# A causal mask that moves from TensorE matmuls to a minimum on VectorE

## The reference

```
qk = x @ W_qk ; q, k = split(qk)            # 16 heads of 64, n = 1024
scores = einsum('bhid,bhjd->bhij', q * 64**-0.5, k)
scores = where(triu(ones(n, n), k=1), -max_float, scores)
attn = softmax(scores)
out = einsum('bhij,bhjd->bhid', attn, k)    # the keys are the values
x = x + out @ W_out
```

## Time and profile before

| | us |
|---|---|
| median of 3 runs (lowest to highest) | 827.27 (824.65 to 827.36) |
| profiled execution: its own time | 827.14 |
| its span, first to last instruction | 825.4 |
| busy: TensorE / VectorE / ScalarE / GpSimd | 740.8 / 462.3 / 390.0 / 439.0 |

### The profile page before, as it was taken

How to read it: one execution, slowest core, us unless ns; L and a number is a source line. 1 busy time by engine, 2 the same in 40 slices (tenths; PEclk the granted TensorE clock), 3 DMA queues, 4 the chain that set the end, 5 groups by cost and what they waited for, 6 DMA issues and landing times. The chain is left out here.

```text
span 825.4 us, 14251 instructions
## 1 busy us (share of the span) xinstructions
PE 740.8 (90%) x5448; PEld 495.9 (60%) x5448; DVE 462.3 (56%) x1232; ACT 390.0 (47%) x483; POOL 439.0 (53%) x316
## 2 busy tenths in 40 slices
PE   2789999999999999999999989988998856679998
PEld 2456555655555565556556547867887522657787
DVE  5765565666556556655755501555455774655343
ACT  2345556555555555555555441355444740255422
POOL 4356775676667658656855680044343553144343
PEclk9699999999999999999999999999999885899999
DMA  2000000000000000000000006132231000033232
GB/s 64 8 1 1 9 1 1 8 1 2 8 1 2 7 2 1 8 2 1 2 1 26 2 1 147 27 120 87 66 104 39 0 1 0 0 106 113 67 106 77
DMA packets 29459, 25.15 MB, mean 30 GB/s; under 512 B 10128, under 2 KB 20944, under 8 KB 29392
## 3 DMA queue, kind: packets, MB, share of 16 engines
q1 hardware_dynamic: 29392, 24.25, 10.1%
HBM read 22.92 MB, written 1.31 MB: 29 GB/s over the span
## 5 line engine op out<-in xcount | busy, mean ns | idle before, releaser
L378 POOL TENSOR_TENSOR all_x<-all_x,at_probs 128x1024 f32<-128x1024 f32 (+3 forms) x128 | 222.9, 1741 | 35.7 <-ACT at_probs L453 21.0
L453 ACT ACTIVATE at_probs<-at_ring 128x1024 f32<-128x1024 f32 x144 | 147.3, 1024 | 113.8 <-PE at_ring L625 107.3
L498 DVE CUSTOM_DVE_ANT_0 at_ring<-at_ring,at_after_query 128x128 f32<-128x128 f32 (+3 forms) x256 | 119.5, 521 | 74.1 <-PE at_ring L590 74.1
L643 PE MATMUL at_out<-at_probs,at_k_nat 128*64 128x512 f32 (+3 forms) x768 | 140.3, 494 | 1.1 <-DVE a_attn_t L521 0.9
L1079 POOL TENSOR_TENSOR m_prod<-m_gate,m_wb 128x512 f32<-128x512 f32 x64 | 81.8, 1283 | 110.6 <-ACT m_gate L936 85.5
L378 POOL TENSOR_TENSOR all_x<-at_probs 128x768 f32<-128x768 f32 (+1 forms) x32 | 66.9, 2091 | 126.5 <-ACT at_probs L453 126.3
L990 DVE TENSOR_TENSOR m_hid<-m_prod,m_u 128x512 f32<-128x512 f32 x64 | 44.0, 687 | 88.7 <-POOL m_prod L1079 84.4
L643 PEld LDWEIGHTS at_out<-at_probs,at_k_nat 128*64 128x64 f32 x768 | 49.2, 136 | 69.9 <-issue 66.0
L494 DVE TENSOR_REDUCE at_half_max<-at_ring 128x2 f32<-128x1024 f32 x64 | 75.5, 1222 | 12.4 <-PE at_ring L590 12.4
L936 ACT ACTIVATE m_gate<-m_g 128x512 f32<-128x512 f32 x72 | 42.9, 599 | 82.2 <-PE m_g L847 81.7
L855 PEld LDWEIGHTS m_acc<-rest_wd,m_hid 128*128 128x128 f32 x576 | 75.9, 194 | 6.2
(11 more groups left out here) (196 smaller groups left out, 1293.4 us busy)
## 6 DMA issues: line engine op xcount, KB each, us to landing
m_wb<-m_wt_far SPq DMA_DIRECT2D x128, 128.0 KB, 2.9
all_x<-in_L_attn_a_x SPq DMA_DIRECT2D x8, 256.0 KB, 3.7
at_w_raw<-in_L_attn_a_W_qk SPq DMA_DIRECT2D x8, 128.0 KB, 2.6
out<-all_x SPq DMA_DIRECT2D x4, 256.0 KB, 2.3
a_room<-in_L_attn_a_W_out SPq DMA_DIRECT2D x1, 512.0 KB, 4.0
m_raw_wg<-in_L_ffn_experts_wg SPq DMA_DIRECT2D x1, 512.0 KB, 4.8
m_raw_wu<-in_L_ffn_experts_wu SPq DMA_DIRECT2D x1, 512.0 KB, 4.2
rest_wd<-in_L_ffn_experts_wd SPq DMA_DIRECT2D x1, 512.0 KB, 4.2
```

Source lines behind the costliest of these rows:

```text
L378: return pool.tensor_tensor(sums[:, :, a * P:b * P], left, right, ALU.add)
L453: act.activation(probs[:, :, slot * BANK:(slot + 1) * BANK], pair("S", unit, slot)[:, :, :], ACT.Exp, scale=BETA).then_inc(exp_done, 1)
L498: last = dve.tensor_tensor_reduce(out=sums_ps, in0=sums_ps, in1=after_query[:, BANK - w:BANK], scale=1.0, scalar=MASKED, op0=ALU.add, op1= ...
L643: last = pe.matmul(out_ps[rows(l), o:o + (b - a) * P], k_nat[g % 3][:, j, rows(l)], probs[:, l, at:at + (b - a) * P], start=(j == 0), stop ...
```

## The change

Nothing is added to the scores any more. The tiles `eye2` and `mask2` go, and a constant tile `cap` of [128, 128] f32 is made at the start: 3e38 where the query isn't before the key, 0 elsewhere. After the exponential of a slot with a diagonal block, VectorE takes the minimum of that block's probabilities (both heads, [128, 2, 128]) and `cap`, in place. A new semaphore `capped` counts the slots so treated; `add_up` and `outputs` wait for it. VectorE does slot 0 in round 0, slot 1 after the first maxima of round 1, slot 2 after the maxima of round 2, and slots 7 and 8 in round 4 between `scale_out` and `max_rows`. The denominators of the first half and their inversion move from round 3 to round 4.

```diff
+DIAGONAL = [slot for slot in range(NSLOT) if any(a == j for j, a, _ in SLOTS[slot])]
...
-        eye2, mask2 = s.sb("eye2", [P, 2, P], BF16), s.sb("mask2", [P, 2, P], BF16)
+        cap = s.sb("cap", [P, P])
...
+        capped = s.sem("capped")
...
+        def caps(unit, slot):
+
+            return len(DIAGONAL) * unit + sum(d <= slot for d in DIAGONAL)
...
         def set_up(pool):
             split_w(pool, 0)
-            pool.memset(eye2[:, :, :], 0.0).then_inc(consts, 1)
-            pool.memset(mask2[:, :, :], 0.0).then_inc(consts, 1)
+            pool.memset(cap[:, :], -MASKED).then_inc(consts, 1)
             pool.memset(neg_pick[:, :], 0.0).then_inc(consts, 1)
             pool.memset(after_query[:, :], 0.0).then_inc(consts, 1)
-            pool.wait_ge(consts, 4)
+            pool.wait_ge(consts, 3)
...
+            pool.affine_select(out=cap[:, :], in_=cap[:, :], compare_op=ALU.is_ge, fill=0.0,
+                               base=0, pattern=[[1, P]], channel_multiplier=-1).then_inc(consts, 1)
...
             for l in range(2):
-                pool.affine_select(out=eye2[rows(l), :, :], in_=eye2[rows(l), :, :], compare_op=ALU.not_equal, fill=1.0,
-                                   base=0, pattern=[[DH, 2], [-1, P]], channel_multiplier=1).then_inc(consts, 1)
-                pool.affine_select(out=mask2[rows(l), :, :], in_=mask2[rows(l), :, :], compare_op=ALU.is_ge, fill=MASKED,
-                                   base=0, pattern=[[DH, 2], [-1, P]], channel_multiplier=1).then_inc(consts, 1)
...
                 def add_up(unit, n):
 
                     pool.wait_ge(exp_done, NSLOT * unit + SUM_NEEDS[n] + 1)
+                    pool.wait_ge(capped, caps(unit, SUM_NEEDS[n]))
...
-                        if r == 3:
+                        if r == NBURST - 1:
                             invert(unit, 0)
...
+                def cap_diagonal(unit, slot):
+
+                    dve.wait_ge(exp_done, NSLOT * unit + slot + 1)
+                    for seg, (j, a, _) in enumerate(SLOTS[slot]):
+                        if a == j:
+                            own = part(slot, seg, a, a + 1)
+                            last = dve.tensor_tensor(own, own, cap[:, :].unsqueeze(1).to_broadcast([P, 2, P]), ALU.min)
+                    last.then_inc(capped, 1)
...
                             if unit:
                                 scale_out(unit - 1, 0)
+                            cap_diagonal(unit, 0)
                             if more:
                                 queries_low(unit + 1)
                         for what, m in row:
                             if what == "M" and more:
                                 maxima(unit + 1, m)
+                            if (what, m) == ("M", 0):
+                                cap_diagonal(unit, 1)
+                        if r == 2:
+                            cap_diagonal(unit, 2)
                         if r == NBURST - 1:
                             if more:
                                 join_maxima(unit + 1)
                             if unit:
                                 scale_out(unit - 1, 1)
+                            cap_diagonal(unit, 7)
+                            cap_diagonal(unit, 8)
                             if more:
                                 max_rows(unit + 1)
...
-                        for h in range(2 if a == j else 0):
-                            for l in range(2):
-                                pe.matmul(to[l][:, 0:P], mask2[rows(l), h, :], eye2[rows(l), h, :], start=False, stop=False)
...
                     pe.wait_ge(exp_done, NSLOT * g + max(slot for slot, _ in BURSTS[r]) + 1)
+                    pe.wait_ge(capped, caps(g, max(slot for slot, _ in BURSTS[r])))
...
-                        if r == 3:
+                        if r == NBURST - 1:
                             denominators(unit, 0)
```

More of the change, by code:

```diff
@@ L524, in _ @@
                 queries_low(0)
-                dve.wait_ge(consts, 11)
+                dve.wait_ge(consts, 7)
                 for m in range(NMAX):
@@ L661, in _ @@
                 turn_keys(0)
-                pe.wait_ge(consts, 11)
+                pe.wait_ge(consts, 7)
                 pe.wait_ge(cleared, 4)
```

## The result

| us | before | after |
|---|---|---|
| median of 4 (lowest to highest) | 827.32 (824.65 to 829.17) | 864.50 (862.95 to 865.83) |
| profiled execution: its own time | 827.14 | 865.08 |
| its span | 825.35 | 863.33 |

The kernel became slower: 1.0436 times the time before (1.0416 to 1.0457). The prediction was 844.6, range 818 to 852. The direction is as forecast and so are the waits on VectorE, GpSimd and TensorE; the size is twice the forecast, mainly because the granted clock of TensorE also fell, which the forecast doesn't have.

What follows compares the result with a forecast made beforehand. PE was taken to bound the kernel, busy 28.32 of a unit's 28.76 us. Added to 827.14: units 1 to 13 +10.9, unit 0 +3.2, unit 14 +2.4, last unit +1.0, together 17.5, giving 844.6 us, range 818 to 852.

Steps and rivals of the forecast that it cites:

- the masks' price on PE: Mask matmuls on PE: 0.18 to 0.19 us per 512-wide block, 1.40 us a unit.
- M3: Fill 3 of the maxima on PE: starts 0.70 us early; t counts from the unit's first score matmul.
- cap 2: VectorE's minimum on slot 2, behind the maxima of round 2: ends at t = 14.93.
- sum 7: Step 7 of GpSimd's eleven sums: ends at t = 25.26, with no hole left between sums.
- cap 7: VectorE's minimum on slot 7: blocked at the SBUF port by sum 7, about 1.6 us long, ending at t = 25.54.
- sum 8: Step 8 of GpSimd's eleven: gets in between the halves of cap 8, t = 25.7 to 28.1.
- cap 8: VectorE's two minima on slot 8: second half waits for sum 8, about 2.4 us, to t = 28.4, delaying m_rows.
- Rivals 1, 2 and 3: VectorE holds port through cap 8: 816-824, 0.18; no port conflict: 808-816, 0.08; gains and losses cancel: within 4 of 827, 0.07.
- rival 4: The masks' gap on PE is refilled, nothing saved up to M3, the chain 0.70 later: 854 us, chance 0.06.
- Unit 0: Attention's first unit, without older outputs on PE: VectorE-GpSimd chain ends near 29.1 instead of 25.9 us, +3.2.
- The last unit: Attention's end, where PE waits for GpSimd's last sum: sums end about 1 us later, +1.0.
- Units 1 to 13: 13 x 0.84 = 10.9: Steady attention units: PE waits for m_rows, so each takes 29.6 instead of 28.76 us, +0.84.

Runs made afterwards that it cites:

- e1: Kernel before, with the mask matmuls left out and nothing in their place (output not the reference's): 813.98 us, 0.984.
- e2: Changed kernel with 14 extra 512-column matmuls on PE ahead of each unit's first scores: 849.45 us, 1.026.
- e5: Kernel before, masks kept, with m_rows delayed by eight reductions of a constant on VectorE: 861.82 us, 1.0405.
- e9: e5 with one more reduction, of 128 elements, ahead of max_rows: 868.05 us (857.93 to 875.81).
- e10: e5 with a ninth 512-element reduction: 881.78 us (876.14 to 900.2).
- e3: Changed kernel with slot 8's two minima in one VectorE instruction: 828.65 us, 1.0003.
- e8: Changed kernel, each slot's minima in one instruction, slot 2's earlier, sum 8 waiting for cap 8, second half's denominators and inversion in round 2: 815.46 us, 0.9846.
- e6: e3 with the second half's denominators and their inversion moved from round 1 to round 2: 816.01 us, 0.9848.
- e4: Changed kernel with m_rows computed ahead of the minima of slots 7 and 8 on VectorE: 842.24 us, 1.0177.

## Why the prediction was wrong

- Right: the masks' price on PE. From L640 to what follows L642 a 512-wide masked slot now takes 0.46 us (forecast 0.47), and M3 starts at t = 11.50 (11.36). PE was not ready as early as forecast, though: at t = 28.1 (29.89 - 1.79), not 27.7, and e1 says that of the 1.05 us a unit that PE could have gained only 0.88 would have stayed.
- Right: the minimum at 0.41 to 0.42 us (0.42); cap 2's end at t = 15.07 (14.93); sum 7's end at 25.58 (25.26); cap 7's end at 25.87, 1.92 us long (25.54, "about 1.6"); sum 8 between the halves of cap 8 in every unit, from 26.00 to 28.43 (25.7 to 28.1); m_rows' end at 29.84 (29.55); PE waiting 1.8 us (1.9; this agreement is in part luck, as m_rows ends 0.3 us later than forecast and PE is ready 0.4 us later). Rivals 1, 2 and 3 are out by this, and rival 4 by the 0.46. The Trainium skill, page "SBUF — State Buffer", section "Who interferes with whom", has issue order decide and the first to issue hold the port for its whole length; the trace agrees (222.04 before 222.16, 2.43 us whole).
- Small misses: cap 2 ends 0.14 us late and GpSimd's gaps between sums are 0.17 us, not 0.14, so that sum 7 ends 0.3 us late; the steady unit is +1.14 without the clock, not +0.84: 3.9 us in 13 units. Unit 0 (+3.0 for 3.2) and unit 14 (+2.8 for 2.4) hold. The last unit was given +1.0 and took +4.3: its sums start 1.9 us later than before, and it has two stretches at half clock, behind a wait of 3.35 us for m_rows and one of 4.04 for the scaling. In e2, without the first of these stretches and with 3.4 us instead of 6.8 in the other, the last unit is 1.6 us longer than before; so some 2.7 of the 4.3 go with the clock.
- **The step that failed:** "Units 1 to 13: 13 x 0.84 = 10.9." It measured 27.8. The term prices PE's new wait at its length and lets the work behind it run as in the window of before, "at full granted clock". In 8 of the 14 units 1 to 14 the granted clock was 0.50 for 3.4 us or more behind that wait, which cost 1.5 us a unit (2.4 in unit 1). e2 shows it by itself: the same chain on VectorE and GpSimd, the same 29.9 us, the wait filled, no alternation, and 15 us less. With that term added (13.0 in these units, some 2.7 in the last) the sum would have been about 860; the 3.9 above are most of what is then left.
- A sign of it stood in the earlier trace rows: the window of unit 0, with PE busy 23.81 of 25.90 us, has a mean clock of 0.94, beside 1.00 in a unit without holes. I read the busy times of that row and not its clock. The trace of before also shows where in that window: right behind the one wait of PE for m_rows, 2.6 us long, the granted clock is 0.51 for 3.4 us, after 1.00 in the 3.3 us before. PE's wait (total, times, longest), then that window:

```profile
PE at_ring L616 <- DVE at_m_rows L512: 2.6, 1, 2.6
...
42.50:45.90 3.40, 3.40 (x15) 2.15 (x16) 0.00 (x0) 0.91 (x1) 0.00 (x0) 0.51 0.00 0
```

  The profile of before couldn't give the frequency, but it could give a bound: 0.06 x 25.9 = 1.55 us lost in that window, and as much at each of the 15 waits would have put the range's high end near 844.6 + 23 = 868.

The Trainium skill, page "TensorE: Matmul & The Clock Gate", section "HAM oscillation — how this bites in real kernels", tells of a kernel where a wait between groups of matmuls throws the clock back to its lower level at every group. The traces here agree in kind, but not in "every": 9 of 15 waits in the changed kernel, 3 of 15 in e5.

What stays open is what decides which waits are followed by a fall. It isn't the length alone: waits of 1.6 us were followed by a fall in 2 of 13 units (e5), of 1.8 in 7 of 13 with the masks gone and in none of e9's profiled execution, of 2.2 in 3 of 12 (e10). Nor is it the absence of the masks alone (units 2 to 14 of e1, e3 and e8 have no such wait and no fall). No run moves a wait of one length in time, so it is untested whether its moment matters.

## What to carry to other kernels

Price a new wait on TensorE twice: its length, and the stretch at half clock that may follow; here the stretches cost 13.0 us in 13 units, nearly as much as all the rest of the change there (14.8 us: the waits' 23.5, less what PE gained), and where a wait can't be avoided, work that is thrown away may be cheaper than idling (e2). Between two short VectorE instructions that read SBUF twice, a long GpSimd sum that has just been released gets in: put them in one instruction, or release the sum behind them (e3, e8). A change that looks bad in its net time can hold a good part: the mask on VectorE is 1.5% faster than on TensorE (1.3 to 1.8, by the intervals of e6 and e8) once two details of order are mended.

## What the runs showed of the hardware

- After waits of PE of 1.6 to 4.0 us the granted clock was 0.50 for 3.4 us in some cases (6.8 at some waits of 2.6 us and more), in which 512-column matmuls take 0.63 us instead of 0.40; 3.4 us of it cost a unit 1.5 us. Waits of 0.92 and 0.46 us in one unit (e4) were followed by none.
- Whether it happens varies from wait to wait within one execution: of the 13 waits of 1.62 to 1.65 us in e5, two were followed by a fall. Whether it varies from execution to execution isn't shown; the four executions of the changed kernel agree within 2.9 us.
- Two minima of 256 elements back to back cost 0.41 and 2.58 us with a sum released between them, one of 512 costs 0.68, with the sum behind it 2.71 instead of 2.43.
